# Expert slots with weight quantization: the mask in a PSUM bank, a fifth weight buffer, another order of steps

## The reference, cut to what matters

```
x = x + tanh(g_xattn[0]) * gated_adjacency(ctx, layernorm(x))          # stage A
x = x + tanh(g_ffn[0])   * moe(layernorm(x))                           # stages A and B
x = x + tanh(g_xattn[1]) * attention(layernorm(x), ctx, ctx)           # stage C
x = x + tanh(g_ffn[1])   * mx_ffn(layernorm(x))                        # stage D

moe:    8 experts, 2 per token, silu(x @ w1) * (x @ w3) @ w2 with I = 352, plus one shared expert
mx_ffn: silu(q(x) @ q(gate_w).T) * (q(x) @ q(up_w).T), then q(h) @ q(down_w).T
q(t):   per 32 elements of a row: s = max(|t|) / 448;  q = fp8_e4m3(t / s) * s
```

## Time and profile before

| what | us |
|---|---|
| median of 3 runs | 1772.19 (1771.68 to 1775.64) |
| the profiled execution | 1777.08 |
| its span, first to last instruction | 1775.5 |
| mean granted TensorE clock over the span | 0.935 of full |
| busy: PE / DVE / ACT / POOL | 1500.4 / 1283.3 / 750.4 / 468.6 |

### The profile page before, as it was taken

The page is one execution under the profiler, slowest core; times in us unless marked ns, Lnnn a source line. Parts: engine busy times, 40 slices in busy tenths (PEclk is TensorE's granted clock), DMA queues, the critical chain, the costliest instruction groups (busy, mean ns, idle before and its releaser), DMA issues.

```text
span 1775.5 us, 24197 instructions
## 1 busy us (share of the span) xinstructions
PE 1500.4 (85%) x8186; PEld 720.3 (41%) x8186; DVE 1283.3 (72%) x2202; ACT 750.4 (42%) x1316; POOL 468.6 (26%) x438
## 2 busy tenths in 40 slices
PE   2278687891889998459989999998899999999998
PEld 1144444551555555312223233222444544544544
DVE  6887778636899999499988788874655555555555
ACT  5263535223444444327767777775122222222221
POOL 4212111101566666431000000000233233233222
PEclk7589898995999999769999999999999999999999
DMA  5211212114355555366210302126000000000000
GB/s 170 73 43 51 78 49 64 54 32 139 116 168 177 173 172 160 116 144 122 43 27 1 61 0 35 20 49 124 19 1 0 24 0 0 24 0 0 24 12 13
DMA packets 115030, 114.29 MB, mean 64 GB/s; under 512 B 59448, under 2 KB 87352, under 8 KB 114944
## 3 DMA queue, kind: packets, MB, share of 16 engines
q1 hardware_dynamic: 108896, 94.10, 19.3%
q0 software_dynamic: 5760, 18.88, 4.1%
q10 hardware_dynamic: 288, 0.20, 0.1%
HBM read 59.53 MB, written 31.46 MB: 51 GB/s over the span
## 4 chain that ended last, share of the span: by engine, by line
PE 56%; DVE 28%; DMA 5%; issue 4%; ACT 4%; SPq 1%; POOL 1%; DVEq 0%; ACTq 0%; POOLq 0%
PE PS L1971 18%; PE PS L1994 9%; PE PS L830 7%; PE PS L1435 5%; PE PS L1424 5%; PE PS L1415 4%; DVE WORK L1562 4%; PE PS L845 3%; DVE WORK L1813 2%; DVE WORK L1831 2%; DVE WORK L1814 2%; PE PS L1984 2%; ACT BIG L1333 1%; DVE WORK L1805 1%; DMA WORK<-in_L_ffn_down_w_dram 1%
## 5 line engine op out<-in xcount | busy, mean ns | idle before, releaser
L1971 PE MATMUL PS<-BIG 128*128 128x512 f16 x1536 | 340.5, 382 | 8.8 <-DVE BIG L2049 4.6
L1562 DVE TENSOR_REDUCE WORK<-PS 128x2 f32<-128x1024 f32 x256 | 304.4, 1218 | 48.4 <-PE PS L1415 47.8
L1333 ACT ACTIVATE BIG<-PS 128x512 f32<-128x512 f32 x512 | 278.5, 598 | 102.9 <-PE PS L1424 102.8
L1971 PEld LDWEIGHTS PS<-BIG 128*128 128x128 f16 x1536 | 151.0, 98 | 189.7 <-issue 7.8
L1415 PE MATMUL PS<-BIG 128*128 128x512 f16 x512 | 200.2, 398 | 27.7 <-DVE WORK L1562 18.8
L1424 PE MATMUL PS<-BIG 128*128 128x512 f16 x512 | 196.0, 385 | 7.6 <-ACT BIG L1333 3.0
L830 PE MATMUL PS<-BIG,WORK 128*128 (+1 forms) x1152 | 182.6, 316 | 4.8 <-DVE WORK L865 4.8
L1994 PE MATMUL PS<-BIG 128*128 128x512 f16 x768 | 173.8, 379 | 1.8 <-DVE BIG L2069 1.8
L1907 ACT ACTIVATE WORK<-PS 128x512 f32<-128x512 f32 x64 | 38.2, 597 | 304.9 <-PE PS L1971 304.9
L2049 DVE SCALAR_TENSOR_TENSOR BIG<-PS,WORK 128x512 f32<-128x512 f32 x64 | 44.1, 690 | 138.8 <-ACT WORK L1907 138.8
L1435 PE MATMUL PS<-BIG 128*32 128x512 f32 x1024 | 136.0, 604 | 3.8
(11 more groups left out here) (244 smaller groups left out, 2283.5 us busy)
## 6 DMA issues: line engine op xcount, KB each, us to landing
wdq_scratch<-WORK SPq DMA_DIRECT2D x48, 256.0 KB, 3.5
WORK<-in_L_ffn_w_dram SPq DMA_DIRECT2D x32, 352.0 KB, 3.6
y_scratch<-WORK SPq DMA_DIRECT2D x40, 256.0 KB, 2.9
BIG<-BIG SPq DMA_DIRECT2D x96, 64.0 KB, 2.3
X<-in_x_dram SPq DMA_DIRECT2D x4, 1024.0 KB, 9.0
WORK<-in_L_ffn_w_dram SPq DMA_DIRECT2D x16, 256.0 KB, 3.1
WORK<-in_L_ffn_gate_w_dram SPq DMA_DIRECT2D x16, 256.0 KB, 3.8
WORK<-in_L_ffn_up_w_dram SPq DMA_DIRECT2D x16, 256.0 KB, 3.7
```

The source lines that it names most:

```text
L1333: nc.scalar.activation(PB[:, tp, 2 * h + j, :], BBANK[j], ACT.Exp, scale=SOFT_SCALE).then_inc(exp_ok, 1)
L1562: v.tensor_reduce(MXU[:, g % 2, c:c + 2], APAIR[h % 2], AX_X, ALU.max, negate=True).then_inc(max_ok, 1)
L1971: ins = nc.tensor.matmul(bank[b], fxT[:, p, a, k * P:(k + 1) * P], w[:, c, l, k, :], start=(i == 0), stop=(i == 3 * KD - 1))
```

## The change

- The two masks `we` in SBUF become one in PSUM bank 7, in float32. `w_size` waits for `w_second` of the unit before rather than of the one two before.
- Results of all slots go through bank 6; `pe_y` waits for `y_out` of the slot before.
- `wst` has five buffers, and SP loads five units ahead.
- SP stores units and issues loads before it waits for the slot's rows.
- The units' steps stand in another order on ACT, DVE and POOL. A slot's second unit (`[1:]`) has places of its own.
- `const_ok` is merged into `ident_ok` (waits for 2), and stage C's PE waits for all `w_second` before it writes bank 7.

```diff
@@ a_tensor, a_vector, b_constants
-            pe.wait_ge(const_ok, 1)
+            pe.wait_ge(ident_ok, 2)
-            dve.wait_ge(const_ok, 1)
+            dve.wait_ge(ident_ok, 2)
-            g.nop().then_inc(const_ok, 1)
+            g.nop().then_inc(ident_ok, 1)
@@ b_sync
             for i in range(SLOTS):
                 p = i % 2
-                sp.wait_ge(MO.y_out, i + 2)
-                sp.dma_start(y_dram[i * P:(i + 1) * P, :], yo[:, p, :]).then_inc(yst[p], 16)
                 for n in units(i - 1):
                     w_store(sp, n)
                     if n + WBUF < UNITS:
                         w_load(sp, n + WBUF)
+                sp.wait_ge(MO.y_out, i + 2)
+                sp.dma_start(y_dram[i * P:(i + 1) * P, :], yo[:, p, :]).then_inc(yst[p], 16)
@@ b_gpsimd
-                for n in units(i):
+                for n in units(i - 1)[0:1]:
+                    w_back(pool, n)
+                for n in units(i)[0:1]:
                     w_scale(pool, n)
-                for n in units(i - 1):
+                for n in units(i - 1)[1:]:
                     w_back(pool, n)
+                for n in units(i)[1:]:
+                    w_scale(pool, n)
@@ b_scalar, slot
+                for n in units(i - 2)[1:]:
+                    w_hi(act, n)
+                for n in units(i - 1)[0:1]:
+                    w_size(act, n)
                 act_sil(act, MO, HOME, p, i, p)
                 if not (last and p == 1):
                     act_hi(act, MO, HOME, 1 - p, i + 1)
-                for n in units(i - 2):
+                for n in units(i - 1)[1:]:
+                    w_size(act, n)
+                for n in units(i - 1)[0:1]:
                     w_hi(act, n)
-                for n in units(i - 1):
-                    w_size(act, n)
@@ b_scalar, y_out
-                nc.scalar.activation(yo[:, p, :], bank[6 + p][:, :], ACT.Copy).then_inc(MO.y_out, 1)
+                nc.scalar.activation(yo[:, p, :], bank[6][:, :], ACT.Copy).then_inc(MO.y_out, 1)
@@ b_tensor, mfinish
-                if not first:
-                    pe.wait_ge(MO.y_out, i)
-                pe_y(MO, HOME, p, slot, bank[6 + p], True, True).then_inc(MO.y_mm, 1)
+                pe.wait_ge(MO.y_out, i + 1)
+                pe_y(MO, HOME, p, slot, bank[6], True, True).then_inc(MO.y_mm, 1)
@@ b_vector, slot
+                for n in units(i - 2):
+                    w_low(dve, n)
+                for n in units(i - 1)[0:1]:
+                    w_second(dve, link, n)
                 dve_hid(dve, MO, HOME, p, i, p)
                 if not (last and p == 1):
                     dve_lo(dve, MO, HOME, 1 - p, i + 1)
-                for n in units(i):
+                for n in units(i)[0:1]:
                     w_first(dve, link, n)
-                for n in units(i - 2):
-                    w_low(dve, n)
-                for n in units(i - 1):
+                for n in units(i - 1)[1:]:
                     w_second(dve, link, n)
+                for n in units(i)[1:]:
+                    w_first(dve, link, n)
@@ c_tensor
             pe.wait_ge(MO.y_out, SLOTS + 1)
+            pe.wait_ge(QW.n_ok, UNITS)
@@ buffers
-        WBUF = 4
-        wst = carve(WORK, "wst", 28928, [P, WBUF, D])
+        WBUF = 5
+        wst = carve(WORK, "wst", 27136, [P, WBUF, D])
-        we = [carve(WORK, "we0", 37120, [P, D], BF16), carve(WORK, "we1", 27520, [P, D], BF16)]
+        we = bank[7]
-        fw_in = [sem(f"fw_in{i}") for i in range(4)]
+        fw_in = [sem(f"fw_in{i}") for i in range(WBUF)]
@@ w_second
-            link(v.scalar_tensor_tensor(q, we[n % 2], LEAST, q, ALU.max, ALU.add))
-            v.scalar_tensor_tensor(q, we[n % 2], LEAST, q, ALU.max, ALU.subtract).then_inc(QW.n_ok, 1)
+            link(v.scalar_tensor_tensor(q, we, LEAST, q, ALU.max, ALU.add))
+            v.scalar_tensor_tensor(q, we, LEAST, q, ALU.max, ALU.subtract).then_inc(QW.n_ok, 1)
@@ w_size
-            if n >= 2:
-                act.wait_ge(QW.n_ok, n - 1)
-            nc.scalar.activation(we[n % 2], wst[:, n % WBUF, :], ACT.Abs, scale=2.0 ** 20).then_inc(QW.up_ok, 1)
+            if n >= 1:
+                act.wait_ge(QW.n_ok, n)
+            nc.scalar.activation(we, wst[:, n % WBUF, :], ACT.Abs, scale=2.0 ** 20).then_inc(QW.up_ok, 1)
```

More of the change, by code:

```diff
@@ L773, in build @@
         y_dram = nc.dram_tensor("y_scratch", [SLOTS * P, D], F32, kind="Internal").ap()
-        const_ok = sem("const_ok")
         gatew_in = sem("gatew_in")
```

## The result

The changed kernel took 1759.10 us (median of 5 runs, 1752.46 to 1763.13), the kernel before 1772.31 (median of 5, 1771.68 to 1775.64). The ratio of the runs is 0.9899, with a 95% interval of 0.9877 to 0.9921, which is 18 us; that of the two medians is 0.9925, 13 us, outside this interval. The forecast was 1747, its range 1740 to 1761: the time lies in the range, near its upper end, and by the medians the gain is 13 of the 25 us that were forecast. One execution of the kernel before, beside e1 to e4, took 6677.75 us and is in none of the ratios.

The account below looks back on a forecast made before the run. DVE was taken to set the pace in the expert slots: eleven periods going from 21.65 to 19.4 us save 24.8, with 0.8 at the ends 25.6, against a median of 1772.2, giving 1747 us; range 1740 to 1761.

Parts of the forecast that it names:

- DVE was the bound, through collisions: In the expert slots DVE sets the pace; the PSUM mask brings `w_second` to 2 x 0.692 us, saving 2.48 a period.
- `w_size` into PSUM: ACT's `w_size` writing the mask to PSUM keeps its price of 0.615 us, at most twice that.
- Rows through one bank: At `pe_y`, waiting for the `y_out` of the slot before has 2.8 us spare and costs 0.
- POOL's order: POOL's fetch, back, scale, back, scale with waits take 17.0 us a period, inside 18.9.
- the merged semaphore: `const_ok` into `ident_ok` is the same instruction at the same moment and costs 0.
- Five buffers and SP's order: DVE's 3.8 us of waits for loads go, but lie already in its gaps, so no separate gain.
- The third slot: In a period's third slot `dve_lo` ends at 6.8 us where 6.6 was wanted; 0.55 a period was taken for slips.
- Long `w_low`s: DVE's `w_low`, with both inputs in SBUF, keeps its long cases beside POOL; the sum kept its mean of 0.884 us.
- Store behind `w_hi`: ACT's `w_hi` waits 0 to 1.8 us for a store in one slot of three, most often nothing.
- DVE stays near the bound: Rival: `w_low` collisions and the tight third slot make a period 20.5 us and the kernel 1759; chance 0.20.
- What was to show it: Signs in the slots: `w_second` at 690 ns, DVE under 90%, PE over 95%, W13 matmuls 6.4 to 6.5 us apart.

Follow-up runs that it names:

- e1: The changed kernel with PE reading the expert number at the slot's start; ratio to the kernel before 0.9822, a period 19.65 us.
- e4: The changed kernel with the two masks back in SBUF and four weight buffers (new orders alone); ratio to the kernel before 0.9995, a period 21.29 us.
- e10: The changed kernel with POOL's two multiplications per unit replaced by memsets over the same bytes; 1755.78 us in one run, a period 19.85 us.
- e3: The kernel before with only the mask in PSUM bank 7 and rows out through bank 6; ratio to before 0.9959, a period 21.34 us.
- e7: The changed kernel with four weight buffers instead of five; ratio to the kernel before 0.9892, a period 20.19 us.
- e2: The changed kernel with `w_size` ahead of `w_hi`, `w_second` ahead of every `w_low`, the second unit's `w_low` behind `dve_lo`; ratio to before 0.9940.
- e5: The changed kernel with the expert number read ahead, `w_size` ahead of `w_hi`, the second unit's `w_low` behind `dve_lo`; 1745.33 us, ratio to before 0.9819.
- e6: The changed kernel with `w_size` ahead of `w_hi` and the second unit's `w_low` behind `dve_lo`; 1752.30 us, ratio to before 0.9856.

## Why the prediction was right, and where its sizes were off

- **DVE was the bound, through collisions: right.** `w_second` fell to 0.670 and 0.691 us against 2 x 0.692 forecast. That the cause is two SBUF inputs on DVE against POOL's multiplications is shown by e10 for `w_low`, and by e3, with the mask as the only edit on DVE, for `w_second`. The Trainium skill's rule ("SBUF — State Buffer", Who interferes with whom) says the same, and e10's 0.68 us beside a writing POOL is its other half. The dearer PSUM access of DVE that the Trainium skill states ("Perfetto Trace Analysis", Optimizing Scalar/DVE Operations) does not show: `w_second`'s first instruction is 670 ns with the mask in PSUM here and 670 in SBUF in e4.
- **`w_size` into PSUM: right.** 0.597 us, 0.018 less than into SBUF.
- **Rows through one bank, POOL's order, the merged semaphore: right, 0.** PE never waits at `pe_y` (idle 0.0).
- **Five buffers and SP's order: the size right, the reason incomplete.** DVE's waits for loads are gone, but with four buffers too (e7). And SP's order is no option but a need of ACT's new order; the prediction gave it a price and missed the circle.
- **The third slot: mechanism right but for one link, one term wrong.** The prediction had `dve_lo` end 6.8 us into the slot; it ended at 6.75. So close a hit has luck in it: what held `w_second` last was not `w_size` but the second `w_low`, with a collided one ahead of it, and the two ended within 0.2 us of each other. It then said "where 6.6 was wanted", with "handoffs 0.04, an assumption". That is the step that failed: from `dve_lo` to the W13 matmuls it is 0.79 to 0.84 us, as the expert number is loaded between (e1 brings it to 0.14). So it was wanted at 5.8. The slot lost 0.95 us rather than 0.2, and the middle slot, which was to lose nothing, 0.27. The sum is 1.28 us a period over PE's 18.87, and 0.55 was allowed: 11 x 0.73 = 8.0 us of the 25.6. e1 took 0.50 a period of it back. The number was in sight: in the chain of waits of before, PE stood 0.8 to 1.0 us between `dve_lo` and the W13 matmuls in the first two slots, where it waited for it:

```profile
439.06 0.99 issue
...
448.50 0.79 issue
```

- **Long `w_low`s: right in kind, short in size.** The sum kept 0.884 us; it became 1.003, since 23 of the 48 are long where 12 were. 12 of them stand behind `w_back`, which starts as `w_second` of the second unit ends, and 11 behind `w_scale`. The prediction looked at how long a collision is, not at who starts first.
- **Store behind `w_hi`:** rightly nearly nothing here, and the real danger of any further move (e2).
- **The rivals.** By its period (20.15, against 20.5) and its time (1759.1, against 1759) the result is near "DVE stays near the bound". By its mechanism it is not: DVE is 90% busy, and PE waits for a late instruction and a register load. Only in e5 and e6, at 96%, is DVE near the bound.
- **What was to show it.** `w_second` at 690 ns, DVE under 90% (89.9%), PE over 95% (96%), no wait at `pe_y` and some long `w_low`: all there. The W13 matmuls were to be 6.4 to 6.5 us apart and are 6.72 in the mean. Of the signs of being wrong, PE's wait in the third slots came to 0.8 us, where "over 1 us" was named.
- **The whole time.** The slots gave 16.4 us of the 25.6; the rest of the profiled execution gave back 2.5 (2.1 behind slot 36, 0.4 ahead of slot 3). It stood 4.0 above its own median, that of before 4.8.

## What to carry to other kernels

When a change frees one engine, look for where the next wait will fall on the engine that becomes the bound, and at what stands between that wait and its first instruction: a register load behind it costs nothing until the wait is the last one to be met. A reorder and a faster operation can each be worth a fifth of what they are worth together, so neither is to be judged alone. Where DVE and POOL share work on SBUF, place DVE's two-input instructions beside POOL's transfers, or so that they start ahead of POOL's multiplications, and not right behind the instruction that releases POOL; or take one of the inputs from PSUM.

## What the runs showed that was not expected

- The kernel outside the slots, the same instructions in every run that quantizes the weights, differs by some us between profiles: from slot 36 to the end of the span it took 1071.9 (e5) to 1076.6 us (after). It is why a period, read from the trace, tells more here than the whole time. Up to slot 3 it took 456.7 us in e1 and 463.3 in the changed kernel. Of these 6.6 us the slots explain 2.0, with the wait ahead of slot 0. At 308 us e1 stood 1.0 us behind, and by 324 us it was 4.4 ahead. Between the two lies a collision of the same kind, ahead of the slots. In the changed kernel two of DVE's two-input instructions meet POOL's L255 and take 2.5 us more than in e1, and PE waits 2.5 us longer. Timelines of DVE and PE, the changed kernel, then e1:

```profile
302.57 1.97 DVE L581 SCALAR_TENSOR_TENSOR WORK<-WORK 128x512 f32<-128x512 f32 x1
...
310.99 1.36 DVE L589 TENSOR_TENSOR WORK<-WORK 128x4 f32<-128x4 f32 x1
...
312.61 0.18 PE L421 MATMUL PS<-WORK,ONES 128*128 128x4 f16 x1 [4.00 <-DVE WORK L590]
...
314.13 4.00 PE L844 MATMUL PS<-BIG 128*128 128x512 f16 x9 [1.34 <-DVE X L640]
```

```profile
303.53 0.69 DVE L581 SCALAR_TENSOR_TENSOR WORK<-WORK 128x512 f32<-128x512 f32 x1
...
310.67 0.16 DVE L589 TENSOR_TENSOR WORK<-WORK 128x4 f32<-128x4 f32 x1
...
311.09 0.18 PE L421 MATMUL PS<-WORK,ONES 128*128 128x4 f16 x1 [1.52 <-DVE WORK L590]
...
312.61 2.10 PE L844 MATMUL PS<-BIG 128*128 128x512 f16 x9 [1.34 <-DVE X L640]
```

  Behind PE's longer idle time the granted clock stood at half, the 1.2 GHz level, where it was in full in e1. The same nine matmuls took 4.00 us for 2.10, and the clock cost 2.9 us in all before it was back. Busy time from 314 to 320 us, the changed kernel, then e1 (the clock is the third number from the end):

```profile
314.00:320.00 6.00, 5.87 (x17) 2.75 (x18) 4.98 (x11) 0.49 (x1) 0.00 (x0) 0.50 0.07 28
```

```profile
314.00:320.00 6.00, 6.00 (x43) 4.13 (x41) 4.39 (x10) 1.81 (x4) 0.00 (x0) 1.00 0.18 46
```

  The thirteen other traces all have an L581 of 1.97 us or more there, those with e1's edit too, so it is e1's luck and not its edit. In the changed kernel this L581 started 0.09 us behind POOL's L255, in e1 0.25 us ahead of it.
- POOL's multiplications got faster too, 1.14 to 1.05 us. By e3 the mask is not the reason: with the mask alone moved, `w_scale` takes 1.285 us, as `w_low` there starts 0.16 us ahead of it most times. It is the new order, in which POOL always starts first, and DVE pays.
- A load of one number from SBUF into a register of PE's sequencer takes 0.31 us, its arithmetic 0.15 and 0.02 more; with the addresses worked out from it, 0.8 us passed before the first matmul.
